# Row transfers spread over the stage of experts on slots in a new order, and one prepared tile at a time on VectorE between its masks

## What is computed

```
q, k, v = proj(Wq), proj(Wk), proj(Wv)          # 16 heads of width 8
q = _l2norm(q); k = _l2norm(k)
sim = einsum('bhid,bhjd->bhij', q, k) * 8.0      # causal mask, softmax over j
o = einsum('bhij,bhjd->bhid', softmax(sim), v)   # then times Wo
...
top_v, top_i = top_k(softmax(x @ Wr.T), 2)       # top_v made to sum to 1
for e in range(8):
    h = gelu(x @ W1[e].T + b1[e])                # 128 -> 512
    out += (h @ W2[e].T + b2[e]) * w_e           # 512 -> 128, w_e is 0 for all but 2 experts
```

## Time and profile before

| | us |
|---|---|
| median of 3 runs (lowest, highest) | 902.03 (901.43, 902.82) |
| the profiled execution: its own time | 902.33 |
| its span, first to last instruction | 900.3 |
| busy in the span: TensorE | 761.9 |
| VectorE | 505.7 |
| ScalarE | 497.0 |
| GpSimd | 437.6 |

### The profile page before, as it was taken

How to read it: one execution, slowest core, us unless ns; L and a number is a source line. 1 busy time by engine, 2 the same in 40 slices (tenths; PEclk the granted TensorE clock), 3 DMA queues, 4 the chain that set the end, 5 groups by cost and what they waited for, 6 DMA issues and landing times. The chain is left out here.

```text
span 900.3 us, 19314 instructions
## 1 busy us (share of the span) xinstructions
PE 761.9 (85%) x6148; PEld 449.8 (50%) x6148; DVE 505.7 (56%) x1315; ACT 497.0 (55%) x833; POOL 437.6 (49%) x553
## 2 busy tenths in 40 slices
PE   3777577888888898799999999999988878889774
PEld 2656222223322332599999999999523223233222
DVE  6798863365355446344444444444477675766643
ACT  2665365666666675344444444444666666657572
POOL 3444258887788878100000000000487787886884
PEclk9888686889888988899999999999798997989988
DMA  7656483334343434342222222222234433543421
GB/s 206 222 192 216 107 200 80 99 79 105 81 111 79 105 87 83 89 136 70 70 70 70 70 70 70 70 70 69 61 82 99 101 89 84 102 97 86 86 60 41
DMA packets 170117, 89.20 MB, mean 99 GB/s; under 512 B 77104, under 2 KB 159824, under 8 KB 170064
## 3 DMA queue, kind: packets, MB, share of 16 engines
q1 hardware_dynamic: 161872, 71.74, 31.5%
q0 software_dynamic: 8192, 16.79, 7.1%
HBM read 39.47 MB, written 32.24 MB: 80 GB/s over the span
## 5 line engine op out<-in xcount | busy, mean ns | idle before, releaser
L626 ACT ACTIVATE prob<-psum 128x1024 f32<-128x1024 f32 x320 | 312.3, 1033 | 184.9 <-PE psum L722 182.5
L747 PE MATMUL psum<-prob,v 128*18 128x384 f32 (+2 forms) x2560 | 210.1, 429 | 63.6 <-DVE prob L1141 29.2
L526 POOL TENSOR_SCALAR_AFFINE_SELECT prob<-prob 128x512 f32<-128x512 f32 x128 | 89.1, 698 | 309.0 <-ACT prob L626 308.2
L638 ACT ACTIVATE prob<-psum,prob 128x256 f32<-128x256 f32 x284 | 117.3, 470 | 148.2 <-PE psum L877 147.3
L722 PE MATMUL psum<-qks 32*128 32x512 f16 (+3 forms) x1024 | 132.3, 328 | 22.9 <-ACT prob L626 17.0
L515 POOL DMA_INDIRECT slot_x<-rows,idx x128 | 129.0, 1008 | 44.9 <-issue 35.6
L513 POOL DMA_INDIRECT rows<-slot_y,idx x128 | 127.4, 995 | 44.4 <-issue 37.2
L889 PEld LDWEIGHTS psum<-prob 128*128 128x128 f32 x1136 | 137.9, 192 | 3.6
L877 PE MATMUL psum<-rows,prob 128*128 128x256 f32 x568 | 135.9, 383 | 2.8 <-DVE rows L1249 2.8
L889 PE MATMUL psum<-prob 128*128 128x128 f32 x1136 | 138.1, 275 | 0.0
L722 PEld LDWEIGHTS psum<-qks 32*128 32x128 f16 x1024 | 34.8, 95 | 177.9 <-ACT prob L626 106.5
(11 more groups left out here) (118 smaller groups left out, 721.5 us busy)
## 6 DMA issues: line engine op xcount, KB each, us to landing
rows<-slot_x SPq DMA_DIRECT2D x71, 128.0 KB, 2.2
slot_y<-rows SPq DMA_DIRECT2D x71, 128.0 KB, 1.8
xs<-in_L_attn_x SPq DMA_DIRECT2D x16, 256.0 KB, 3.3
prob<-in_L_ffn_W SPq DMA_DIRECT2D x16, 256.0 KB, 3.1
xn_rows<-xns SPq DMA_DIRECT2D x16, 256.0 KB, 3.7
xn_cols<-xts SPq DMA_DIRECT2D x16, 256.0 KB, 3.7
xt<-xn_cols SPq DMA_DIRECT2D x16, 256.0 KB
rows<-xn_rows SPq DMA_DIRECT2D x16, 256.0 KB, 3.0
```

The lines of the kernel that those rows point to most:

```text
L526: pool.affine_select(out=p, in_=p, compare_op=ALU.is_ge, fill=0.0, base=0, pattern=[[0, 2], [0, 2], [1, P]], channel_multiplier=-1).then_i ...
L626: act.activation(prob[:, q % 2, KEPT[u], :], score[(q + u) % 2], ACT.Exp, scale=SCALE / UP ** 2).then_inc(exp_done, 1)
L638: act.activation(hs[:, s, c, :], psum[:, 2 * s + c // 2, (c % 2) * FT:(c % 2 + 1) * FT], ACT.Gelu, bias=ws[:, s, B1C + c:B1C + c + 1]).the ...
L747: mm = pe.matmul(ps_o[32 * g:32 * g + VW, first:first + cols], lhs, prob[:, w % 2, KEPT[u], c:c + cols], start=(i == 0 and not odd), stop= ...
```

## The change

**Half of the row transfers go to the stage of experts.** In bodies 0 to 7 only the rows of batches 0 to 7 are scattered, one batch per body, 8 DMAs, one behind each of the eight groups of masks. The rows of batches 8 to 15 are scattered by a loop of GpSimd's in `between`, while the first tiles of the experts are computed. The slots are laid out anew so that this can be: first the tiles that are filled by rows of batches 0 to 7 alone, expert by expert, then the tiles that both halves share, then the rest. Tiles below EARLY = 25 hold only rows of the first half; the rows of the first half lie in tiles below COVER = 39. SyncE waits for all scatters ahead of `load_tile(25)`. After tile 38 is stored, GpSimd gathers the results of batches 0 to 7, still under the experts, and VectorE combines them from step BACK0 = 46 to 69, 8 instructions in three steps. Bodies 8 to 15 gather and combine batches 8 to 15, 8 gathers in each body and, one body later, 8 combines; the last body combines batch 14 and its own. The tiles of the experts (`xg`, `xgt`, `ys`) lie in `xs` now, as `rows` is in use.

**VectorE prepares tile 0 in quarter 0, tile 1 in quarter 1, tiles 2 and 3 in quarter 2.** TensorE's projections move with them. `v` has two buffers and is written by `prepare` itself, so `copy_v` and `vn` are gone. 

**The arithmetic of the slots is longer** (three lists of ends instead of one, and the ranks of each half are placed with a comparison and a jump), and the expert of each tile now comes from four small instructions, one matmul on `pick` and a copy (`write_plan`) instead of eight instructions over all tiles. SyncE stores two finished batches of the output at the end of a body instead of its beginning. 71 tiles are computed as before.

```diff
+    EARLY = (TOPK * HALF * N - E * (FT - 1) + FT - 1) // FT
+    COVER = (TOPK * HALF * N + E * (FT - 1)) // FT
+    BACK0 = COVER + 7
+    MOVES = TB * TOPK
...
-        vn = sb("vn", [P, TB * H, DH])
-        v = sb("v", [P, TB * H, VW])
+        v = sb("v", [P, 2, TB * H, VW])
...
             def between():
                 for j in range(2):
-                    sp.wait_ge(moved[j], 16 * TB * TOPK * HALF)
+                    sp.wait_ge(moved[j], 8 * MOVES * HALF)
                 for k in range(3):
                     load_tile(k, k % 2)
+                load_rows(HALF + 1, 1)
 
                 def step(k, s):
+                    if isinstance(k, int) and k + 3 == EARLY:
+                        for j in range(2):
+                            sp.wait_ge(moved[j], 8 * MOVES * NB)
                     if not isinstance(k, int) or k + 3 < FFN_TILES:
                         load_tile(k + 3, 1 - s)
                     if not known(k, 0):
...
-                expert_tiles(sp, step)
+                    if isinstance(k, int) and k % 3 == 1 and HALF + 1 + k // 3 < NB and k > 3:
+                        load_rows(HALF + 1 + k // 3, (HALF + 1 + k // 3) % 2)
...
-                        order = [0], [1, 2], [3], [4], [5], [6, 7], [], []
+                        order = [0], [1], [2], [3], [4], [5], [6], [7]
                         if known(b, 0):
                             order = [], [], [], [0, 1], [2, 3], [4, 5], [6], [7]
-                        for k in order[slot]:
-                            move(b, k // TB, k % TB, second)
-            attention(pool, body, lambda: None)
+                        if last:
+                            order = [0, 1], [2, 3], [4, 5], [6, 7], [], [], [], []
+                        for o in order[slot]:
+                            move(b, par, o, second)
+
+            def between():
+                with pool.Fori(HALF // 2, NB // 2) as i:
+                    for j in range(2):
+                        for o in range(MOVES):
+                            move(2 * i + j, j, o, False)
+                for s in range(2):
+                    pool.wait_ge(y_out[s], 16 * ((COVER + 1 - s) // 2))
+                for j in range(2):
+                    for o in range(MOVES):
+                        move(j, j, o, True, early=True)
+                with pool.Fori(1, HALF // 2) as i:
+                    for j in range(2):
+                        for o in range(MOVES):
+                            move(2 * i + j, j, o, True, early=True)
+            attention(pool, body, between)
...
-                    if some(b):
-                        dve.wait_ge(v_ready, b)
+                    if some(NQ * (b - 1)):
+                        dve.wait_ge(pv_done, NQ * (b - 1))
...
+            def combine(m, j, part):
+
+                for o in part:
+                    c, t = o // TB, o % TB
+                    if o == part[0]:
+                        count = counted_by(dve, 8 * MOVES * (NB + m - j) + 16 * MOVES)
+                        dve.wait_ge(made, 1)
+                        dve.wait_ge(moved[j], count)
...
             def body(b, par, second=False, last=False):
-                each = TB * TOPK
                 for w in range(NQ):
                     n = NQ * b + w
                     if not (w == 0 and (known(b, 0) or known(b, HALF))):
                         mask2(n - 1, (w - 1) % NQ)
                     if w == 0:
-                        if not known(b, 0):
-                            copy_v(b)
                         if not last:
-                            prepare(b + 1, 0)
-                            prepare(b + 1, 1)
+                            scale_of(b + 1)
+                            prepare(b + 1, 1 - par, 0)
                     elif w == 1:
                         if not known(b, 0):
                             divide(2 * b - 1, 1)
+                        if not last:
+                            prepare(b + 1, 1 - par, 1)
                         if not known(b, 0):
                             dve.wait_ge(ontr_done, b)
                             if some(b - 1):
                                 dve.wait_ge(outp_done, b - 1)
                             dve.tensor_copy(ot, ps_pc).then_inc(ot_ready, 1)
-                        if not last:
-                            prepare(b + 1, 2)
                     elif w == 2:
                         if not last:
-                            prepare(b + 1, 3)
+                            prepare(b + 1, 1 - par, 2)
+                            prepare(b + 1, 1 - par, 3)
                     else:
                         if some(b):
                             dve.wait_ge(ontr_done, b)
                         divide(2 * b, 0)
                         if not known(b, 0):
-                            add_attention(b - 1, each * (2 * (b - HALF) + 1) if second else 0)
-                    if second and w >= 2 and not (last and w == 3):
-                        combine(b, w - 2, b - 1 if w == 2 else b)
+                            add_attention(b - 1, MOVES * b if second else 0)
+                    if second and not known(b, HALF) and w in (1, 2):
+                        combine(b - 1, 1 - par, range(MOVES // 2 * (w - 1), MOVES // 2 * w))
+                    if last and w == 3:
+                        combine(b, par, range(MOVES))
+                    if known(b, 0) and w == 1:
+                        write_plan()
...
-                expert_tiles(dve, step)
+                for k in range(4):
+                    step(k, k % 2)
+                with dve.Fori(2, BACK0 // 2) as i:
+                    step(2 * i, 0)
+                    step(2 * i + 1, 1)
+                dve.wait_ge(added, HALF - 1)
+                with dve.Fori(0, HALF // 2) as i:
+                    for h in range(6):
+                        step(BACK0 + 6 * i + h, h % 2)
+                        combine(2 * i + h // 3, h // 3, [(0, 1, 2), (3, 4, 5), (6, 7)][h % 3])
```

294 lines of the change are left out of this document (167 added, 127 removed).

## The result

The kernel after takes 799.39 us (median of 4 runs, 796.57 to 802.14), the kernel before 902.1 us beside it (4 runs, 901.43 to 902.82): a ratio of 0.8861, 95% interval 0.8821 to 0.8902. The profiled execution took 802.14 us, with a span of 800.4. Forecast were 837 us with a range of 815 to 871, so the time lies 16 us under the range. The direction was right, the size was not.

The account below looks back on a forecast made before the run. Attention was taken as a chain of late-mask waits, the experts as bound by TensorE: 902.3 - 58.5 (thirteen bodies) - 13.5 (outside) + 2.5 + 3 + 1 + 1 = 837.8, with the end 837 us; range 815 to 871.

Parts of the forecast that it names:

- The clean body, 25.4 us: Attention: a body with masks on time at full clock takes 25.4 us, from two bodies less listed losses.
- The rest kept per body, 0.6 for masks and 0.7 for the clock: Attention: 0.6 us of mask waits and 0.7 us of clock loss remain, making a body 26.7 us.
- no engine is full ... so it is a chain of waits: Attention: engines are busy below a body's some 30 us; TensorE's mask waits, 63.3 us in all, tell the chain.
- the case that I gave 0.09: Rival, attention bodies: cleaner than thought, no mask waits left and full clock, 815 us; chance 0.09.
- VectorE: Attention: copy_v, 8 of 16 combines in late bodies and one tile ahead go; its mask is 1.7 us earlier.
- Outside of the bodies: Outside the thirteen bodies: three bodies' worth saves 13.5 us, small costs are added; -6.8 us in all.
- The routing: Batch 0, quarter 1: TensorE waits for pick_ready behind longer slot arithmetic; 2.5 us lost, between 0 and 5.
- The wait for tile 25: Experts: late scatters delay the load of tile 25; TensorE waits once, 2.4 us computed, 3 taken.
- The combines: Experts from step 46: three combines of 0.40 us stand ahead of copy_w1; 1 us lost, between 0 and 8.
- A new wait in the body: Rival, attention: ScalarE's exponentials or late transposes limit bodies to 28.4 to 29 us, 870 us; chance 0.24.
- VectorE as the bound of the experts: Rival, experts from step 46: 24 steps lose perhaps 0.8 us each, 20 us, giving 857 us; chance 0.05.
- GpSimd's DMAs slowed by VectorE's copies: Rival, experts: DMAs of 2.2 us add 77 us, giving 914; gain gone from 2.1 us on; chance 0.03.

Follow-up runs that it names:

- the run with the old order of tiles: Kernel after with the old order of VectorE's prepared tiles and TensorE's projections; 808.83 us, ratio 0.8977; on the second kind of chip 903.73 us, 0.9612.
- Clumping: Kernel after with its eight DMAs per body four in a row, twice; 802.96 us, ratio 0.8922; on the second kind of chip 942.58 us, 1.001.
- the memsets: Kernel after plus one, two or three dead memsets before each quarter's first-block mask; ratios 0.8924 (one), 1.0032 and 1.0 (two), 1.0553 (three).
- the run with the moved mask: Kernel before, all transfers kept, with one GpSimd mask per quarter given to VectorE; 943.49 us against 937.6, ratio 1.0074.
- The run with three memsets: Kernel after plus three dead memsets ahead of each quarter's first-block mask from batch 1 on; 991.32 us against 940.0 for the kernel before, ratio 1.0553.

## Why the prediction was wrong, step by step

**The direction and the place were right.** The gain is in the bodies, from masks that come in time, and none of it is lost again among the experts.

**The clean body, 25.4 us, is the step that failed first.** It is 24.35, and 1.05 x 13 makes 14 us. The step took the body of before less what TensorE lists as waits for masks. But TensorE's busy time itself, for the same matmuls at the clock of 1.00, is 24.10 us with such waits and 23.2 without. In the run with the old order of tiles, with 1.9 us of waits in a body, it is 23.50. So a listed wait is short of its price; that matmuls behind it start anew instead of overlapping is my reading, and no run shows it by itself. The early body agreed only because the same 24.10 stood in its sum as the clock's price: 26.86 - 24.10 = 2.8, where 26.86 - 23.2 = 3.7 had to go for the clock and the restarts together. With 23.2 in both sums the late body gives 24.4 us and the early one 24.6. The agreement of the two at 25.4 was no second witness.

How much lay in waits and how much in busy time is read from the windows of the ruler, before and after, with the same number of matmuls in them:

```profile
171.76:359.19 187.43, 161.86 (x1514) 55.69 (x1514) 97.06 (x223) 121.50 (x132) 148.42 (x181) 0.88 0.39 91
664.93:883.26 218.33, 179.02 (x1758) 62.30 (x1757) 139.98 (x346) 141.99 (x154) 170.51 (x211) 0.91 0.39 87
```

```profile
160.32:306.40 146.08, 139.31 (x1514) 53.18 (x1514) 91.79 (x216) 120.98 (x132) 96.34 (x127) 1.00 0.41 86
616.34:786.63 170.29, 159.53 (x1758) 60.65 (x1757) 113.17 (x282) 140.94 (x154) 113.92 (x150) 1.00 0.41 91
```

TensorE's busy time fell by 42.0 us and its idle time by 47.4, in all 89.4. Nearly all of the 47.4 are waits for masks, 47.2 us in these windows before and 1.4 after. Of the 42.0 some 36 are the clock's, an estimate from the busy times and the clocks of the first two rows, 161.86 x 0.12 + 179.02 x 0.09. So a body lost nearly as much by slower matmuls (3.2 us) as by idle time (3.6 us), and the listed waits show only the latter.

**The rest kept per body, 0.6 for masks and 0.7 for the clock, failed as well.** Both are nearly 0: mask waits of 2.0 us in the whole span, clock 1.00 in the bodies shown. 1.3 x 13 makes 17 us. With the 14 above this is the 31 us between 58.5 and 89.4. The clock, at 0.88 and 0.91 in the thirteen bodies before, is 1.00 in all of them now.

**Behind both lies what I read in the first paragraph: "no engine is full ... so it is a chain of waits".** Busy time alone said so, 24 to 25 us of 30 for GpSimd. Its own waits say otherwise: it waited for an input 0.5 and 0.8 us in the two bodies shown, 1.6 us in the mean of thirteen. With this the question would have been how much time is taken off GpSimd, some 11 us (eight DMAs at 1.25 and one index copy with its wait), which leaves 18 to 19, and what is full next: TensorE with 24.1 by the rows of then. The answer would have been the case that I gave 0.09, and 815 us, its end, is still 16 us too slow. Clumping shows that at eight DMAs a body their place doesn't matter, and the memsets that GpSimd's time costs a body without any transfer. That its time is the only bound is refuted, on the second kind of chip, by the run with the moved mask: it took 2.8 us a body off GpSimd, which then wasn't full, and nothing was gained.

**VectorE.** Forecast to be worth about as much as GpSimd's part by the listed waits (29.2 of 63.3 us); it was worth 1.2% alone and 6.4 us on top of the other half. Two thirds of its waits went without its new order. The parts that I costed at nothing (quarter 2 with two tiles and four combines, the late transposes) cost nothing: none of the thirteen bodies has a wait for VectorE's mask or for transposes, and the one for transposes in batch 0, 4.3 us, was there before (4.4).

**Outside of the bodies** -6.8 us was forecast and -10.5 came. The routing was in size: TensorE waits 3.9 us, forecast 2.5, between 0 and 5; the stretch up to the first `add_attention` still gained 11.4. The wait for tile 25 was at the place forecast and mis-sized: 5.6 us against 2.4 computed and 3 taken. The reads of rows paced the scatters, as in my sum: that of batch 10, at tile 4, costs GpSimd 6.4 us, and GpSimd doesn't make it good, since it needs nearly 11 us for a batch and the reads come every 11.2. What the sum had too small is the last stretch. From the read of batch 15 (390.88 us) to the last scatter (405.72) it is 14.8 us and not 12.2, because batch 14 with its gap of 2.23 us and some longer DMAs ended late. The first tile's load costs 3.1 us in a wait, forecast as 1 us more; with the other 5.6 these are the 8.7 us listed. The combines cost 0 (between 0 and 8): from 470 to 585 us TensorE is busy 115.00 of 115.00 us. The end gave 3.3, not 0.8.

**The rivals.** A new wait in the body: refuted on the chips where the result was taken. VectorE as the bound of the experts: refuted, for the same 115.00 us, though VectorE's copies are longer there beside the DMAs of GpSimd (128x640 in 567 ns in the mean, 493 before; 128x516 in 447, 429 before). GpSimd's DMAs slowed by VectorE's copies: the groups of the kernel after have

```profile
L546 POOL DMA_INDIRECT slot_x<-rows,idx x128 | 126.1, 985 | 48.8 <-issue 29.5 <-DMA rows<-xn_rows 10.8 <-ACT prob L674 7.5
L544 POOL DMA_INDIRECT rows<-slot_y,idx x128 | 123.2, 963 | 53.5 <-issue 25.7 <-DVE acc L1248 17.4 <-ACT prob L674 8.6
```

985 ns for a scatter and 963 for a gather, against 1008 before. In a row 0.30 us come on top, 1.3 us in all, where 2.1 would have decided. The section of the Trainium skill cited there (SBUF — State Buffer, Who interferes with whom) also names the converse, that casts of VectorE from SBUF to SBUF can take the shared ports and block or be blocked by a GpSimd instruction as a whole. (The 620 and 3100 ns stand in another section of that page, A bandwidth-pool intuition that's wrong.) The run with three memsets agrees with that: 1.14 us for the cast above against 0.33.

## What to carry to other kernels

Before you call a stage a chain of waits, read for each engine what it waits for, not what it is busy: an engine that hardly ever waits for its input is full, at 80% busy too, and taking waits off its neighbour then mostly renamed them here. But a full engine need not be the only bound: test it by taking other work off it. A clean duration that is got by subtracting listed waits came out too long here; compare TensorE's busy time for the same matmuls with and without waits, and in windows that hold the whole stage, not in two bodies. Where a queue feeds another (the reads of rows, the scatters), follow it from its first element, and measure on more than one chip before a gain of this kind is promised.
